# ScalarE takes gate arithmetic and projection eviction in a graph-attention and mixture-of-experts kernel, and the router's products move to a quarter of a tile

## What is computed

```python
def gnn(x, adj):                        # x is layer-normalized before
    h = x @ W.T + b_W
    e = (h @ a1)[:, None] + (h @ a2)[None, :] + b_a[0]
    e = where(e > 0, e, 0.2 * e)
    scores = where(adj > 0, e, -9e15)
    return softmax(scores, axis=1) @ h
x = x + gnn(layernorm(x), adj)

def ffn(x):                             # 64 experts, the 2 best of each row
    topk_logits, topk_idx = top_k(x @ Wr + br, 2)
    gates = softmax(topk_logits)
    return sum over e of combine[:, e] * (relu(x @ W1[e] + b1[e]) @ W2[e] + b2[e])
x = x + ffn(layernorm(x))
```

## Time and profile before

| | before |
|---|---|
| device time, median of 3 | 280.89 us |
| profiled execution | 280.6 us |
| its span | 278.9 us |
| PE busy | 222.4 us, 80% |
| DVE busy | 218.6 us, 78% |
| ACT busy | 172.0 us, 62% |
| POOL busy | 166.4 us, 60% |
| chain that ended last, by engine | PE 49%, DVE 27%, issue 9%, DMA 7%, POOL 5% |

### The profile page before, as it was taken

How to read it: one execution, slowest core, us unless ns; L and a number is a source line. 1 busy time by engine, 2 the same in 40 slices (tenths; PEclk the granted TensorE clock), 3 DMA queues, 4 the chain that set the end, 5 groups by cost and what they waited for, 6 DMA issues and landing times.

```text
span 278.9 us, 6179 instructions
## 1 busy us (share of the span) xinstructions
PE 222.4 (80%) x1849; PEld 212.8 (76%) x1849; DVE 218.6 (78%) x629; ACT 172.0 (62%) x386; POOL 166.4 (60%) x194
## 2 busy tenths in 40 slices
PE   1493399898968796886985368999999999999840
PEld 1372399798968696786984357999999999999740
DVE  4857989998999989999958733889887766766464
ACT  2743668797666585765751506878877777777400
POOL 5850011634478848888875755444888888866600
PEclk9999579999979999997998556999999999999995
DMA  6993454488474950810991113223148710100067
GB/s 162 227 199 71 79 94 79 82 211 209 139 185 89 285 179 12 292 32 19 374 418 49 59 43 91 66 57 80 42 133 321 256 41 31 40 28 24 31 199 262
DMA packets 11119, 36.88 MB, mean 132 GB/s; under 512 B 2256, under 2 KB 2832, under 8 KB 10320
## 3 DMA queue, kind: packets, MB, share of 16 engines
q0 software_dynamic: 5232, 14.98, 24.6%
q1 hardware_dynamic: 5424, 21.11, 21.6%
q10 hardware_dynamic: 432, 0.40, 0.5%
HBM read 39.36 MB, written 5.51 MB: 161 GB/s over the span
## 4 chain that ended last, share of the span: by engine, by line
PE 49%; DVE 27%; issue 9%; DMA 7%; POOL 5%; ACT 1%; SPq 1%; POOLq 0%; DVEq 0%; ACTq 0%
PE bank L1090 16%; PE bank L1102 15%; DVE arena L693 8%; PE bank L988 6%; DVE arena L699 4%; PE bank L972 4%; POOL table L419 2%; DVE arena L684 2%; DMA arena<-result 2%; DMA xs<-in_x 2%; PE bank L938 2%; DVE xs L705 2%; PE bank L1079 1%; PE bank L948 1%; DVE st L708 1%
## 5 line engine op out<-in xcount | busy, mean ns | idle before, releaser
L988 PE MATMUL bank<-arena 128*128 128x130 f32 x512 | 62.7, 279 | 1.4 <-ACT arena L542 1.3
L988 PEld LDWEIGHTS bank<-arena 128*128 128x128 f32 x512 | 60.3, 194 | 2.1 <-DVE xs L705 1.5
L1090 PE MATMUL bank<-arena 128*128 x384 | 60.4, 281 | 0.1
L1102 PE MATMUL bank<-w2s,arena 128*128 x384 | 58.8, 276 | 0.2 <-issue 0.2
L419 POOL DMA_INDIRECT table<-rows_in,pos x32 | 47.9, 1496 | 11.9 <-issue 8.1
L1090 PEld LDWEIGHTS bank<-arena 128*128 128x128 f32 x384 | 51.2, 194 | 0.5 <-issue 0.2
L1102 PEld LDWEIGHTS bank<-w2s,arena 128*128 128x128 f32 x384 | 50.6, 192 | 0.6 <-issue 0.6
L972 PE MATMUL bank<-ident,arena 128*128 128x128 f32 x256 | 35.5, 299 | 19.0 <-DVE arena L699 19.0
L868 DVE SCALAR_TENSOR_TENSOR arena<-bank,arena 128x128 f32 x96 | 33.6, 350 | 21.7 <-PE bank L1102 20.6
L972 PEld LDWEIGHTS bank<-ident,arena 128*128 128x128 f32 x256 | 32.5, 156 | 20.1 <-DVE arena L699 20.1
L601 ACT ACTIVATE arena<-bank,arena 128x128 f32<-128x128 f32 x96 | 35.1, 366 | 18.1 <-PE bank L1090 16.9
(11 more groups left out here) (190 smaller groups left out, 274.1 us busy)
## 6 DMA issues: line engine op xcount, KB each, us to landing
arena<-in_adj POOLq DMA_DIRECT2D x16, 512.0 KB, 5.4
w2s<-in_w SPq DMA_DIRECT2D x8, 768.0 KB, 4.6
arena<-in_w SPq DMA_DIRECT2D x6, 1024.0 KB, 9.2
arena<-in_w SPq DMA_DIRECT2D x4, 512.0 KB, 4.9
w2s<-in_w SPq DMA_DIRECT2D x4, 512.0 KB, 3.8
xs<-in_x SPq DMA_DIRECT2D x4, 256.0 KB, 6.3
arena<-result SPq DMA_DIRECT2D x2, 512.0 KB, 4.3
arena<-result SPq DMA_DIRECT2D x4, 256.0 KB, 6.1
```

The costliest lines, as they stand in the source:

```text
L988: ins = pe.matmul(OB[t % 2][:, 0:D + 2], pt_r[:, t % 2, j, :], h[:, j, :], start=(j == 0), stop=(j == T - 1))
L1090: ins = pe.matmul(hp(p, b), w1u[:, p % UW, P * b:P * b + P], xT_all[:, bass.ds(column, P)], start=True, stop=True)
L1102: ins = pe.matmul(yp(p), hT[:, p % UH, b, :], w2s[:, bass.ds(u, 1), b, :].rearrange("p e d -> p (e d)"), start=(b == 0), stop=(b == HB - 1))
```

## The change

- ACT computes `gs` = `ge` + 1 behind the exponential (through a bias of ones), and copies the gates into `rows_out` (`route_c` of ACT, signalled by `s_gated`). DVE does neither any more. POOL's `place` waits for `s_gated` too.
- ACT evicts h (a plain copy, 128x258); the bias is added by PE through a matmul of one row of ones with `hbias`, sixteen of them. `s8` comes from ACT in two parts (tiles 0 to 3, then 4 to 15). The last quarter of `xh` is written by DVE instead of ACT. `xhT` moves to another buffer.
- PE runs all four `scores_row` before the first `project`.
- `route_b` of PE comes after a quarter of the tiles in `attend` instead of after half.
- DVE's nine small index instructions move ahead of the statistics; `place(3)` of DVE moves ahead of `residual(14)`; POOL's loads 2 and 3 come after the fourth quarter's statistics; POOL's place for tile 9 comes after rstd_of(6); at the end PE's `route_c(4)` comes ahead of `route_b(5)`.

```diff
@@ -23,7 +23,7 @@
...
     LAST = [START[q + 1] - 1 for q in range(NG)]
-    PLACED = [(0, 0, 8), (0, 1, 9), (0, 2, 10), (0, 3, 11), (1, 4, 12), (1, 5, 13), (1, 6, 13), (1, 7, 14), (2, 8, 15), (2, 9, 15)]
+    PLACED = [(0, 0, 8), (0, 1, 9), (0, 2, 10), (0, 3, 11), (1, 4, 12), (1, 5, 13), (1, 6, 13), (1, 7, 14), (2, 8, 15)]
     LNS = [(t, t + 2) for t in range(0, T - 2, 2)] + [(T - 2, T - 1), (T - 1, T)]
@@ -100,7 +100,7 @@
...
         zl = xT_all[:, 0:TOPK * T * D].rearrange("p (k t d) -> p k t d", k=TOPK, t=T)
-        xh, xhT = z_r[:, 1, :].rearrange("p (t d) -> p t d", t=T), z_r[:, 2, :]
+        xh, xhT = z_r[:, 1, :].rearrange("p (t d) -> p t d", t=T), pt_r[:, 1, :, :].rearrange("p t i -> p (t i)")
@@ -369,6 +373,7 @@
...
+            pool.memset(ones_f1[:, :], 1.0)
             pool.memset(expo[:, :], -0.5)
@@ -393,8 +398,10 @@
...
                 pool.tensor_tensor(nm2[:, ct], nm2[:, ct], rstd[:, ct], ALU.mult).then_inc(s_nm, 1)
-                if c < 3:
-                    load(c + 1)
+                if c == 0:
+                    load(1)
+            load(2)
+            load(3)
@@ -414,6 +421,7 @@
...
+                pool.wait_ge(s_gated, q + 1)
                 pool.wait_ge(s_pos, q + 1)
@@ -445,6 +453,7 @@
...
             rstd_of(6)
+            place(2, 9)
             rstd_of(7)
@@ -511,7 +520,6 @@
...
             scale(2)
-            scale(3)
             trow_evac(0)
@@ -519,11 +527,27 @@
...
+            def h_evac(c):
+                act.wait_ge(s_h, c + 1)
+                act.activation(h[:, 2 * c:2 * c + 2, 0:D + 1],
+                               bank[4 + c % 4][:, 0:2 * (D + 1)].rearrange("p (t d) -> p t d", t=2), ACT.Copy).then_inc(s_hs, 1)
+
+            def slope(t0, t1):
+                act.wait_ge(s_hs, t1 // 2)
+                act.activation(s8[:, t0:t1], h[:, t0:t1, D], ACT.Copy, scale=1.0 - SLOPE).then_inc(s_s8, 1)
+
+            h_evac(0)
+            h_evac(1)
+            slope(0, 4)
+
             def scores(t):
-
-                if t == 0:
-                    act.wait_ge(s_s8, 1)
+                if t == 1:
+                    for c in range(2, 8):
+                        h_evac(c)
+                    slope(4, T)
+                if t in (0, 4):
+                    act.wait_ge(s_s8, 1 + t // 4)
                 act.wait_ge(s_z, t + 1)
@@ -558,6 +582,13 @@
...
                 act.activation(ge[:, 0:n], gd[:, 0:n], ACT.Exp).then_inc(s_ge, 1)
+                act.wait_ge(s_ge, q + 1)
+                act.activation(gs[:, 0:n], ge[:, 0:n], ACT.Identity, bias=ones_f1[:, 0:1]).then_inc(s_gs, 1)
+
+            def route_c(q):
+                rows = slice(START[q], START[q + 1])
+                act.wait_ge(s_gate, q + 1)
+                act.activation(rows_out[:, rows, :, GATE_COL], gate[:, :, rows].rearrange("p k g -> p g k"), ACT.Copy).then_inc(s_gated, 1)
@@ -573,16 +604,22 @@
...
                         route_b(q)
+                    if s == LAST[q] + 5:
+                        route_c(q)
             norm(T - 4)
...
             route_a(5)
+            route_c(3)
             route_b(4)
             norm(T - 1)
+            route_c(4)
             route_b(5)
             route_a(6)
+            route_c(5)
             route_b(6)
+            route_c(6)
@@ -649,14 +686,6 @@
...
-            def h_evac(c):
-
-                dve.wait_ge(s_h, c + 1)
-                dve.tensor_tensor(h[:, 2 * c:2 * c + 2, 0:D + 1],
-                                  bank[4 + c % 4][:, 0:2 * (D + 1)].rearrange("p (t d) -> p t d", t=2),
-                                  hbias[:, :].rearrange("p (t d) -> p t d", t=1).to_broadcast([P, 2, D + 1]),
-                                  ALU.add).then_inc(s_hs, 1)
-
             def xT_evac(b):
@@ -675,6 +704,15 @@
...
+            dve.wait_ge(s_pool, 4)
+            dve.wait_ge(s_set, 1)
+            dve.tensor_scalar(sidx[0:P // 2, :], pidx[0:P // 2, :], 2.0, None, ALU.mult)
+            dve.tensor_scalar(sidx[P // 2:P, :], pidx[P // 2:P, :], 2.0, 1.0 - P, ALU.mult, ALU.add)
+            for into in (r_lo, r_hi, r_blk):
+                dve.tensor_copy(into[E:E + 1, :], iota_p[E:E + 1, 0:TAB])
+            for k in range(1 + TOPK):
+                ins = dve.tensor_scalar(padrow[:, k, ID_COL:ID_COL + 1], pidx[:, :], float(DUMP + (E + (k - 1) * P if k else 0)), None, ALU.add)
+            ins.then_inc(s_rows, 1)
             for c in range(4):
@@ -740,8 +778,7 @@
...
-                dve.wait_ge(s_ge, q + 1)
-                link(dve.tensor_scalar(gs[:, 0:n], ge[:, 0:n], 1.0, None, ALU.add))
+                dve.wait_ge(s_gs, q + 1)
                 link(dve.reciprocal(gate[:, 0, rows], gs[:, 0:n]))
@@ -750,8 +787,6 @@
...
                 link(dve.tensor_reduce(rank[:, :, 0:n], rk[:, :, 0:n, :], AX.X, ALU.add))
-                dve.wait_ge(s_gate, q + 1)
-                dve.tensor_copy(rows_out[:, rows, :, GATE_COL], gate[:, :, rows].rearrange("p k g -> p g k"))
                 dve.scalar_tensor_tensor(pos[:, rows, :].rearrange("p g k -> p k g"), idxf[:, rows, :].rearrange("p g k -> p k g"), float(STRIDE),
@@ -763,29 +798,15 @@
...
             xT_evac(0)
+            penalty(0)
+            dve.wait_ge(s_nm, 4)
+            for t in range(12, T):
+                ins = dve.tensor_scalar(xh[:, t, :], xs[:, t, :], rstd[:, t:t + 1], nm2[:, t:t + 1], ALU.mult, ALU.add)
+            ins.then_inc(s_norm3, 1)
             xT_evac(1)
-            penalty(0)
             xT_evac(2)
-            dve.wait_ge(s_was, 1)
-            h_evac(0)
-            h_evac(1)
             penalty(1)
-            for c in range(2, 6):
-                h_evac(c)
             scores(0)
-            h_evac(6)
-            h_evac(7)
-            dve.wait_ge(s_hs, 8)
-            dve.tensor_scalar(s8[:, :], h[:, :, D], 1.0 - SLOPE, None, ALU.mult).then_inc(s_s8, 1)
-            dve.wait_ge(s_pool, 4)
-            dve.wait_ge(s_set, 1)
-            dve.tensor_scalar(sidx[0:P // 2, :], pidx[0:P // 2, :], 2.0, None, ALU.mult)
-            dve.tensor_scalar(sidx[P // 2:P, :], pidx[P // 2:P, :], 2.0, 1.0 - P, ALU.mult, ALU.add)
-            for into in (r_lo, r_hi, r_blk):
-                dve.tensor_copy(into[E:E + 1, :], iota_p[E:E + 1, 0:TAB])
-            for k in range(1 + TOPK):
-                ins = dve.tensor_scalar(padrow[:, k, ID_COL:ID_COL + 1], pidx[:, :], float(DUMP + (E + (k - 1) * P if k else 0)), None, ALU.add)
-            ins.then_inc(s_rows, 1)
             for s in range(1, T):
@@ -800,8 +821,8 @@
...
             leaky(T - 1)
+            place(3)
             residual(T - 2)
-            place(3)
             top2(4)
@@ -922,7 +943,10 @@
...
             def turn_x(b):
-                pe.wait_ge(s_norm, b + 1)
+                if b < 3:
+                    pe.wait_ge(s_norm, b + 1)
+                else:
+                    pe.wait_ge(s_norm3, 1)
                 for c in range(CB):
@@ -945,20 +969,23 @@
...
                         t = 2 * c + j
-                        ins = pe.matmul(bank[4 + c % 4][:, j * (D + 1):(j + 1) * (D + 1)], xhT[:, P * t:P * t + P],
-                                        wt_s[:, :], start=True, stop=True)
+                        at = bank[4 + c % 4][:, j * (D + 1):(j + 1) * (D + 1)]
+                        pe.matmul(at, xhT[:, P * t:P * t + P], wt_s[:, :], start=True, stop=False)
+                        ins = pe.matmul(at, ones_f[0:1, :], hbias[0:1, :], start=False, stop=True)
                     ins.then_inc(s_h, 1)
...
             pe.wait_ge(s_was, 1)
+            scores_row(0)
+            turn_x(2)
+            scores_row(1)
+            turn_x(3)
+            scores_row(2)
+            scores_row(3)
+            pe.wait_ge(s_set, 1)
             for b in range(4):
-                scores_row(b)
-                if b < 2:
-                    turn_x(b + 2)
-                if b < 3:
-                    project(b)
-            project(3)
+                project(b)
@@ -981,7 +1008,7 @@
...
                     for q in range(NG):
-                        if j == T // 2 and t == LAST[q] + 2:
+                        if j == T // 4 and t == LAST[q] + 2:
                             route_b(q)
@@ -1031,8 +1058,8 @@
...
             route_a(5)
+            route_c(4)
             route_b(5)
-            route_c(4)
             route_a(6)
...
             route_c(5)
```

## The result

The changed kernel takes **294.53 us** in the median (292.87 to 295.44, 4 runs), the kernel before 281.16 us beside it (279.63 to 282.65): ratio **1.047, 95% interval 1.039 to 1.055**. It is slower by 13 us, where no change was forecast. The profiled execution took 292.87 us, 12.3 us more than before; its span is 291.1 us.

What follows compares the result with a forecast made beforehand. It took DVE to bound the tile loop, PE's chain the start, and POOL's DMA issues the gather behind the loop. 280.6 - 6.2 + 4.4 + (0.7 to 1.7) gave 279.5 to 280.5, taken as 280.0 us; range 277.5 to 283.5.

Steps and rivals of the forecast that it cites:

- The row products early: At the start, PE's list loses three of four project ahead of the fourth scores_row; trow whole at about 20.6, 2.7 us earlier.
- 0.89 us for eight instructions is now one pair of tiles: At the start, bias products double PE's work, priced at 0.89 us a pair of tiles; pair 7 done at 27.8.
- Rival 4: At the start, PE does projections at the slow rate, 1.72 us a pair; leaky(2) at 46.2, total 288.8 us; chance 0.12.
- The evictions on ACT: At the start, ACT evicts h at near 0.38 us each, bounded by 0.28 and 0.59.
- the start: Ahead of the loop, leaky(2) starts at 37.4 instead of 41.97: a gain of 4.5 us, ends 3.5 and 5.3.
- The loop: Groups 0 and 1: earlier route_b gains 1.4 us by shorter DVE waits, place 0.25 by DVE's lost add and copy.
- The middle: In the loop, group 1's late gate copy delays POOL's issues; 0.7 to 1.7 us arrive at the last attend's end.
- Rival 2: In the loop, POOL's issues find gaps and no lateness reaches the last attend: 278.8 us; chance 0.12.
- Behind the loop: After the last attend, POOL's issues wait for ACT's copies of groups 3 and 4: loss 4.4 us, ends 3.9 and 5.0.

Runs made afterwards that it cites:

- bias_pair: The changed kernel with one one-row bias product of 258 columns ahead of each pair's two products, instead of one per tile; ratio 1.023 to the kernel before.
- bias_k128: The changed kernel with every bias product made of 128 rows (weights 1/128) instead of one row; ratio 1.008 to the kernel before.

## Why the prediction was wrong, point by point

- **The row products early: right.** `trow` was forecast whole at 20.6 and is at 19.25 + 0.60 = 19.85.
- **The step that failed: "0.89 us for eight instructions is now one pair of tiles".** It priced a one-row product by rows of 128-row products. The eight take 1.66 us at full clock, because of four changes, and 2.9 at the half clock (bias products of 128 rows took 0.89). With that price corrected alone the last pair would have ended at about 19.1 + 8 x 1.66 = 32.4, still 4.6 us past the forecast of 27.8; the clock made it 39.1. The term came out at +6.5 us where -4.5 was forecast: 11.0 of the 12.8 us by which the sum was off.
- **Rival 4 had the outcome and a part of the cause.** It named `leaky(2)` at 46.2 and 288.8 us. What spoke against it, that PE is continuously busy and was fast from 18, didn't hold: PE was busy by the rows, and fast at 18, and the clock still fell at 23.2. Up to there the loss came from the changes, which it doesn't name: its pair of 1.72 us is near the 1.66 measured at full clock by luck, since it stands for a pair without changes at the slow rate.
- **The evictions on ACT: right.** 0.39 us each, forecast 0.38. With 128-row bias products the end of the start's working holds, `leaky(2)` at 37.35 for 37.4. The ratio of that kernel is 1.008, which on 281.2 us makes 283.3 (282.1 to 284.4): with the start as forecast the time would have come out 3 us over the sum, at the upper edge of the range of 277.5 to 283.5. In its trace the middle lost 2.1 us where 1.2 were summed, and the part behind the loop 5.5 instead of 4.4.
- **The loop: right, a little small.** The waits at `lg` of groups 0 and 1 went; 2.2 us gained for 1.65.
- **The middle: mechanism right, place and size wrong.** The rule that what POOL starts inside a DVE pass ends with that pass plus its own time bore out (3.07 us for the issue, 2.55 for the power, 2.58 for an issue at 131.99). The working priced group 1's late copy at 0.7 to 1.7 us, and it costs about 0.3. The loss of 3.8 came from group 0's last tile, of which the working said only that its issues slip at no cost: it took the second `wait_ge` of `place` at nothing. That wait costs 0.24 us there, and the pass began 0.12 us ahead of the issue. The margin stood in the trace of the kernel before, 0.18 us; the working has no row on it, and none on what a second wait costs.
- **Rival 2 fell with it.** The same issue took 3.07 us where it began 0.12 us behind the start of the pass, and 0.98 where it began ahead of it. The Trainium skill, SBUF — State Buffer, section Who interferes with whom, which the prediction weighed, infers that the writing of descriptors is free of such passes. The rows disagree for an indirect issue as a whole; it also reads its addresses `pos` from SBUF, and no run here tells which of its parts was held.
- **Behind the loop: right.** POOL idles for the copy of group 3, issues four DMAs, and rstd_of(8), `norm(15)` and the copy of group 4 follow as forecast; 4.1 us for 4.4.
- With the start at -4.5 and the middle at 1.2 the sum was 280.0; with +6.5, -2.2, +3.8 and +4.1 it is 292.8, and 292.87 was measured.

## What to carry to other kernels

An fp32 matmul with few rows in between others with 128 rows isn't priced by its columns: give a bias 128 rows (weights of 1/128), or collect such products. When POOL runs tightly between long DVE passes, a wait of a quarter of a microsecond can cost a whole pass, so merge semaphores that are waited for together. A small copy moved to another engine costs what stands ahead of it there, if a queue of a third engine waits for it.

## What was not expected of the hardware

- Each change between a 128-row fp32 product and one of 1 or 32 rows took about 0.19 us at full clock. At the half clock it was about 0.3 us: (2.9 - 1.72) / 4 from the changed kernel and (2.31 - 1.72) / 2 from bias_pair, with the 1.72 us of the earlier trace rows for as many instructions without a change at the slow rate. In the rows shown the weight load did not run ahead across a change.
- Such an alternation, begun at 19.05, was followed by a fall of the granted clock from 1.00 to 0.50 at 23.2, with PE busy in all of it by the trace, and the clock stayed there to the end of the alternation at 39.1 and was back at 1.00 from 44 on. The same products without changes (bias_k128) show no fall. All seven traces with changes at every tile or every pair show one, at 22.0 to 25.0. PE's ends are modelled in the profile. The Trainium skill, TensorE: Matmul & The Clock Gate, Part 1, says that the clock is set by how busy PE has been; that the pauses at the changes count as idle in this sense would fit both, and is argued, not shown. What the clock follows stays open in detail: bias_pair, with fewer changes, fell sooner (22 against 23.2), and bias_k128, with a gap of PE of 0.8 us between 24 and 26, did not fall. The clock column itself needs care: it reads 1.00 from 12 us on in the kernel before, where eight instructions at 15.71 took 1.72 us, and 0.89 at 20.85.
- The second of two semaphore waits ahead of a DMA issue of POOL took 0.24 us (0.39 against 0.15); neither row names a semaphore as what was waited for.
